# A scan layer's prelude: the convolution as shifted additions on VectorE, two softplus put behind the first scans

## The reference, cut to what matters

```python
gate = sigmoid(x @ W2 + b2)                     # x is the normed input; W1, W2 are 128 x 256
u = x @ W1 + b1
u_pad = pad(u, 3 zeros ahead of the sequence)
u = sigmoid(sum(u_pad[:, k:k + 512, :] * conv_w[:, k] for k in range(4)) + conv_b)
xp = u @ x_proj_w                               # 64 + 16 + 16 columns
delta = softplus(xp[..., :64] @ dt_proj_w + dt_proj_b)
B, C = xp[..., 64:80], xp[..., 80:]
for each time t:                                # 256 channels, 16 states
    h = exp(delta * A) * h + delta * B * u      # A = -exp(A_log)
    y = sum over the states of h * C
out = (y + u * D_skip) * gate @ Wo + bo
```

## Time and profile before

| | us |
|---|---|
| median of three runs (lowest, highest) | 1510.48 (1509.72, 1516.7) |
| the profiled execution | 1518.01 |
| its span, first to last instruction | 1516.2 |
| TensorE busy in the span | 1255.5 |
| VectorE busy | 1024.5 |
| ScalarE busy | 727.8 |
| GpSimd busy | 627.7 |
| first scan of the first layer starts at | 82.26 |
| last instruction of VectorE in the first layer (L609) ends at | 306.14 |

### The profile page before, as it was taken

The page is one execution under the profiler, slowest core; times in us unless marked ns, Lnnn a source line. Parts: engine busy times, 40 slices in busy tenths (PEclk is TensorE's granted clock), DMA queues, the critical chain, the costliest instruction groups (busy, mean ns, idle before and its releaser), DMA issues. The chain is left out here.

```text
span 1516.2 us, 30869 instructions
## 1 busy us (share of the span) xinstructions
PE 1255.5 (83%) x11646; PEld 684.2 (45%) x11674; DVE 1024.5 (68%) x2274; ACT 727.8 (48%) x1593; POOL 627.7 (41%) x838
## 2 busy tenths in 40 slices
PE   7856677769999988547878989987989699999976
PEld 3312233222333337424656666665767333333276
DVE  3699999978888855357446745545632588988653
ACT  2843334316766675313523614443452166766754
POOL 1378888753425215313423334223332524351244
PEclk9978888869999998757889968988997699999988
DMA  4379833023224022441321131141120231331213
GB/s 120 137 264 375 300 137 140 21 66 86 54 65 111 23 80 62 102 85 23 80 40 29 35 83 20 25 100 21 18 52 10 66 81 28 97 88 45 79 48 89
DMA packets 137738, 128.43 MB, mean 85 GB/s; under 512 B 92007, under 2 KB 123559, under 8 KB 132202
## 3 DMA queue, kind: packets, MB, share of 16 engines
q1 hardware_dynamic: 129536, 118.56, 28.3%
q0 software_dynamic: 2496, 5.13, 1.1%
q10 hardware_dynamic: 5558, 2.76, 0.9%
HBM read 105.61 MB, written 38.62 MB: 95 GB/s over the span
## 5 line engine op out<-in xcount | busy, mean ns | idle before, releaser
L1343 DVE TENSOR_REDUCE f_row_min<-f_ps 128x1 f32<-128x512 f32 x512 | 324.4, 677 | 61.2 <-PE f_ps L1670 61.0
L1233 ACT ACTIVATE f_e<-f_ps 128x512 f32<-128x512 f32 x512 | 282.9, 602 | 131.6 <-PE f_ps L1690 128.6
L1670 PE MATMUL f_ps<-f_operands 72*128 72x512 bf16 x512 | 205.1, 409 | 30.0 <-DMA f_operands<-k_scr 16.1
L1690 PE MATMUL f_ps<-f_operands 75*128 75x512 bf16 x512 | 190.5, 382 | 2.6 <-ACT f_e L1233 2.1
L740 PE MATMUL m_ps<-m_shared,sb_ident 128*128 128x512 f32 x256 | 140.2, 698 | 50.8 <-DVE m_shared L596 49.0
L359 POOL TENSOR_TENSOR m_drive<-m_du,m_ring 128x1024 f32<-128x1024 f32 x64 | 150.9, 2372 | 52.7 <-DVE m_ps L588 33.3
L476 ACT ACTIVATE m_ps<-m_delta,m_A 128x511 f32<-128x511 f32 x128 | 83.0, 681 | 129.5 <-DVE m_ps L588 104.8
L1701 PE MATMUL f_ps<-f_e,f_v_op 128*32 128x512 f32 x1024 | 138.0, 611 | 2.1 <-ACT f_e L1233 1.4
L1670 PEld LDWEIGHTS f_ps<-f_operands 72*128 72x128 bf16 x512 | 51.6, 101 | 185.6 <-DVE f_row_min L1343 130.5
L2495 DVE TENSOR_REDUCE d_row_min<-d_ps 128x1 f32<-128x384 f32 (+3 forms) x176 | 106.3, 633 | 37.8 <-PE d_ps L2736 36.8
L2664 DVE TENSOR_TENSOR d_aT<-d_ps,d_aT 128x16 f32<-128x16 f32 x224 | 37.9, 169 | 138.5 <-PE d_ps L2842 138.1
(11 more groups left out here) (291 smaller groups left out, 2343.5 us busy)
## 6 DMA issues: line engine op xcount, KB each, us to landing
m_ring<-bc_scr SPq DMA_DIRECT2D x32, 1024.0 KB, 6.8
f_rows_scr<-blank SPq DMA_DIRECT2D x2, 8707.5 KB, 33.0
f_wall<-f_wall SPq DMA_DIRECT2D x16, 578.0 KB
f_operands<-q_scr SPq DMA_DIRECT2D x32, 288.0 KB
f_operands<-k_scr SPq DMA_DIRECT2D x96, 96.0 KB
d_q_op<-q_scr SPq DMA_DIRECT2D x6, 576.0 KB
d_k_op<-k_scr SPq DMA_DIRECT2D x18, 192.0 KB
f_operands<-f_rows_scr SPq DMA_DIRECT2D x46, 64.5 KB, 1.8
```

Source lines behind the costliest of these rows:

```text
L1233: nc.scalar.activation(e_sb[:, n % 3, hh, :], ps[:, SCORE[(b * UNITS + u) % SCORE_BANKS], :], ACT.Exp, scale=SCALE).then_inc(s["e_out"], 1)
L1343: nc.vector.tensor_reduce(row_min[:, b % 2, u // TPB, u % TPB:u % TPB + 1], ps[:, MAXQ[(b * UNITS + u) % MAX_BANKS], :], AX.X, ALU.max, ne ...
L1670: nc.tensor.matmul(ps[:, MAXQ[n % MAX_BANKS], :], q_op(b, QK)[:, hd, t * P:(t + 1) * P], k_op(b, QK)[:, hd, :], start=True, stop=True).the ...
L1690: nc.tensor.matmul(ps[:, SCORE[n % SCORE_BANKS], :], k_op(b, QKS)[:, hd, t * P:(t + 1) * P], q_op(b, QKS)[:, hd, :], start=True, stop=True ...
```

## The change

The convolution leaves TensorE. `project_u` becomes one product per half with W1 itself. ScalarE copies the result with the bias b1 from PSUM into `du` (`raw`), VectorE multiplies it by the last tap and adds the other three taps times the shifted columns (`convolve`: two tensor_scalar and six scalar_tensor_tensor of 512 columns per batch, or a few columns fewer), and `inputs` takes the sigmoid from SBUF in place, with conv_b as its bias. The product of weights and taps, the edge product and two loads are gone. The orders of VectorE, ScalarE and TensorE in the prelude are written anew. `softplus(2)` and `softplus(3)` move on VectorE behind the output of step 0, and ScalarE takes the two logarithms ahead of the decays of step 2.

```diff
@@ ScalarE
-                act.dma_start(taps, core.dram["m_taps"].unsqueeze(0).to_broadcast([P, CONV_K * MLP])).then_inc(s["taps_in"], 16)
-                load("m_edge", "taps_in")
+                def raw(b):
+                    act.wait_ge(s["u_ps"], b + 1)
+                    for k in range(HALVES):
+                        last = nc.scalar.activation(du[:, k, tokens(b)], bank(U_IN + k), ACT.Identity, bias=vec(core, "b1", k))
+                    last.then_inc(s["raw_out"], 1)
+
                 def inputs(b):
-                    act.wait_ge(s["u_ps"], b + 1)
-                    act.wait_ge(s["u_bias_out"], 1)
+                    act.wait_ge(s["conv_step"], (b + 1) * CONV_STEPS)
                     for k in range(HALVES):
-                        last = nc.scalar.activation(u[:, k, tokens(b)], bank(U_IN + k), ACT.Sigmoid, bias=u_bias[:, k:k + 1])
+                        last = nc.scalar.activation(u[:, k, tokens(b)], u[:, k, tokens(b)], ACT.Sigmoid, bias=vec(core, "conv_b", k))
                     last.then_inc(s["u_out"], 1)
@@ ScalarE's list, after the change
+ turned(0) raw(0) gates(0) turned(1) raw(1) inputs(0) turned(2) raw(2) gates(1) turned(3) raw(3) inputs(1) steps(0)
+ gates(2) decline(0) steps(1) logarithm(0) inputs(2) inputs(3) gates(3) decline(1) steps(2) logarithm(1) steps(3)
+ decline(2) decline(3), then the decays, with
+                        if step == DEFERRED_AT + 1:
+                            for later in DEFERRED:
+                                logarithm(later)
@@ VectorE
+                def convolve(b):
+                    done = b * CONV_STEPS
+                    dve.wait_ge(s["raw_out"], b + 1)
+                    for back in range(CONV_K):
+                        for k in range(HALVES):
+                            tap = vec(core, "conv_w", k * CONV_K + CONV_K - 1 - back)
+                            if back == 0:
+                                nc.vector.tensor_scalar(u[:, k, tokens(b)], du[:, k, tokens(b)], tap, None,
+                                                        ALU.mult).then_inc(s["conv_step"], 1)
+                            else:
+                                dve.wait_ge(s["conv_step"], done + (back - 1) * HALVES + k + 1)
+                                held = u[:, k, b * S + back:(b + 1) * S]
+                                nc.vector.scalar_tensor_tensor(out=held, in0=du[:, k, b * S:(b + 1) * S - back], scalar=tap, in1=held,
+                                                               op0=ALU.mult, op1=ALU.add).then_inc(s["conv_step"], 1)
@@ VectorE's list, after the change
+ norm(0) skip_weights() A norm(1) convolve(0) norm(2) convolve(1) projections(0) norm(3) projections(1) convolve(2)
+ one_plus(0) convolve(3) projections(2) softplus(0) one_plus(1) projections(3) softplus(1) memset
+ one_plus(2) one_plus(3), then the scans, with
+                    if step + 1 == DEFERRED_AT:
+                        for later in DEFERRED:
+                            softplus(later)
@@ TensorE
                     if b >= 1:
-                        pe.wait_ge(s["u_out"], b)
+                        pe.wait_ge(s["raw_out"], b)
                     for k in range(HALVES):
-                        for j in range(CONV_K):
-                            nc.tensor.matmul(bank(U_IN + k), tap_W[:, j, cols], xnT[b % 2][:, j:j + S], start=(j == 0), stop=False)
-                        last = nc.tensor.matmul(bank(U_IN + k)[:, 0:CONV_K - 1], edge_w[:, cols], edge[:, 2 * MLP:],
-                                                start=False, stop=True)
+                        last = nc.tensor.matmul(bank(U_IN + k), W1[:, k * P:(k + 1) * P], xnT[b % 2][:, CONV_K - 1:],
+                                                start=True, stop=True)
@@ TensorE's list, before, then after the change (u, gate, rows, dt: project_u, project_gate, project_rows, project_dt)
- turn(0) u(0) turn(1) gate(0) u(1) turn(2) rows(0) gate(1) dt(0) u(2) turn(3) rows(1) gate(2) dt(1) u(3) rows(2) gate(3)
- dt(2) rows(3) dt(3)
+ turn(0) u(0) gate(0) turn(1) u(1) turn(2) u(2) gate(1) rows(0) turn(3) u(3) dt(0) gate(2) rows(1) dt(1) gate(3) rows(2)
+ dt(2) rows(3) dt(3)
```

More of the change, by code:

```diff
@@ L263, in mamba_phase @@
         W1, W2, Wx, Wdt, Wo = (core.w[n] for n in ("m_W1", "m_W2", "m_xp", "m_dt", "m_Wo"))
-        taps, edge = ring[:, RING - 1, 0, :, :].rearrange("p r s -> p (r s)"), core.w["m_edge"]
         f_hn = gate[:, 0, 0:S].rearrange("p (t h) -> p t h", t=TPB)
@@ L441, in _ @@
                 turned(0)
+                raw(0)
+                gates(0)
+                turned(1)
+                raw(1)
                 inputs(0)
-                turned(1)
-                gates(0)
+                turned(2)
+                raw(2)
+                gates(1)
+                turned(3)
+                raw(3)
                 inputs(1)
-                turned(2)
-                gates(1)
                 steps(0)
+                gates(2)
                 decline(0)
+                steps(1)
                 logarithm(0)
                 inputs(2)
-                turned(3)
-                gates(2)
-                steps(1)
-                decline(1)
-                logarithm(1)
                 inputs(3)
                 gates(3)
+                decline(1)
                 steps(2)
+                logarithm(1)
+                steps(3)
                 decline(2)
-                steps(3)
                 decline(3)
-                logarithm(2)
-                logarithm(3)
                 act.wait_ge(s["a_ready"], 1)
@@ L552, in _ @@
                 norm(0)
-                taps_and_biases()
+                skip_weights()
                 dve.wait_ge(s["a_exp"], 1)
@@ L556, in _ @@
                 norm(1)
+                convolve(0)
                 norm(2)
+                convolve(1)
                 projections(0)
                 norm(3)
+                projections(1)
+                convolve(2)
                 one_plus(0)
-                projections(1)
+                convolve(3)
+                projections(2)
                 softplus(0)
                 one_plus(1)
-                projections(2)
+                projections(3)
                 softplus(1)
-                projections(3)
                 dve.wait_ge(s["gate_out"], B)
                 nc.vector.memset(ps[:, 0:2 * HALVES * S].rearrange("p (a s) -> p a s", s=S)[:, :, 0:1], 0.0).then_inc(s["decay_zeroed"], 1)
-                one_plus(2)
-                one_plus(3)
-                softplus(2)
-                softplus(3)
+                for later in DEFERRED:
+                    one_plus(later)
                 dve.wait_ge(rows_out[B - 2], 16)
@@ L2967, in build @@
         mamba_weights = ExitStack()
-        later = ("in_L0_attn_a_x", "ones", "pad", "f_wall", "blank", "m_taps")
+        later = ("in_L0_attn_a_x", "ones", "pad", "f_wall", "blank")
         for name, a in sorted(arrays.items(), key=lambda item: item[0].startswith("m_")):
```

69 lines of the change are left out of this document (29 added, 40 removed).

## The result

The changed kernel takes 1521.82 us (median of 4 runs, 1517.97 to 1527.16), the kernel before in the same session 1510.1 (4 runs, 1508.06 to 1516.7). The ratio is 1.0082, with an interval of 1.0047 to 1.0117: 0.8% slower. The forecast was 1525.2.

The account below looks back on a forecast made before the run. Layer end was taken as first-scan start plus VectorE's full list behind it. First scan +4.8, moved softplus +7.4 and collision +2.5 gave +14.7 us: 1532.7 for the profiled execution, 1525.2 for the median, range 1512 to 1531.

Parts of the forecast that it names:

- The first scan at 87.0: End of the prelude, from stepping through the engines' queues: first scan at 87.0 us against 82.26, +4.8 us.
- softplus(1) fits in before, to 80.3: VectorE late in the prelude: softplus of batch 1 ends at 80.3 us, before one_plus(3) ends at 87.0.
- Five slow bursts worth 7.2 together: TensorE's prelude: lower-clock products on the path cost 7.2 us; at the upper clock the first scan comes at 79.9.
- Rival (a): TensorE's prelude: gaps stay short and the clock holds, -2.4 + 9.9 = +7.5 us, total 1518.0; chance 0.17.
- (c): Prelude and scans: first scan at 79 to 82 us, GpSimd out of the way, total 1511 to 1517; chance 0.16.
- (d): Prelude: convolutions at their upper price and slow products throughout, total 1531 to 1535; chance 0.10.
- Everything later waits for norm(3): Prelude queues: turn(3) and raw(3) stand ahead of other batches' work, so all later work waits for norm(3), ending at 40.2.
- Convolution 4.4 to 4.5 us per batch: VectorE's prelude: each batch's convolution costs 4.4 to 4.5 us (4.4 to 5.3), 18 in all.
- Softplus moved: +7.4, collision +2.5 (0 to 3.7): Behind the first scan: six products of batches 2 and 3 add 7.4 us to VectorE, colliding with GpSimd for 2.5.
- Logarithms and table loads between decays at nothing: ScalarE between decays of steps 1 and 2: two logarithms and two table loads, 4.7 us, hidden beside VectorE's work.
- Rival (b): Prelude: VectorE runs almost without waiting, first scan at 62.3 us, -10 us, total 1500.4; chance 0.07.
- Whatever moves the first scan moves the end by as much: Scan stretch: VectorE's list is full from the first scan, so any shift of it passes fully to the layer's end.

Follow-up runs that it names:

- the kernel with the clock held: Changed kernel with TensorE's prelude gaps filled by 52 unused products up to the next real product; first scan 82.12 us, layer end 315.47 us.
- the reordered kernel: Changed kernel with VectorE, ScalarE and TensorE prelude queues in other orders and no deferral of softplus and logarithms; ratio 0.9981 to the kernel before.
- the run with one tap: Changed kernel with three of the four convolution taps left out, 16 us less VectorE work; first scan 2.45 us earlier.
- after: The changed kernel as profiled, against the kernel before; median 1521.82 us, ratio 1.0082.
- The reordered kernels: Changed kernel with new queue orders and no deferral: alone (0.9981), with GpSimd's bias additions later (1501.07 us), and also with drives 1 to 3 delayed (first scan 68.72 us).
- the drives held back: New queue orders, no deferral, later bias additions, plus GpSimd's drives 1 to 3 waiting for the last softplus; first scan 68.72 us, layer end 296.58 us.

## Why the prediction was right

The time was forecast as 1525.2, +14.7; measured is +11.7 in the medians and +13.9 at the end of the layer. Sign and size came out, by the mechanism that was called likeliest. Luck has a part in how closely: the clock alone moved the copy for batch 1 from 50.94 to 56.63 us between executions, and the mis-sized terms below partly cancel. By its steps:

- **"The first scan at 87.0" (+4.8): 87.59.** The way there was right too. The copies for batches 0 to 3 stand at 32.35, 50.94, 65.80 and 73.95 where the walk has 32.8, 51.1, 65.6 and 74.5. (The sign given for it, VectorE idle some 5 us ahead of the copies of batches 0 and 1, did not fit the walk itself, which has 4.9 and 10.9; measured are 3.5 and 11.3.) The last link was partly another: the walk ends through ScalarE's decline(3), but one_plus(2) starts at 83.83, when the last stretched product of softplus(1) ends, half a microsecond after decline(2) at 83.3.
- **"softplus(1) fits in before, to 80.3": mis-sized.** Its three products took 2.17, 3.25 and 3.25, 5.0 us of stretching for some 1.0 allowed. It ended at 83.9. VectorE, idle in the walk, is full from 65.8 us on. It cost only 0.6 us here because ScalarE was just as late; in the kernel with the clock held it is what keeps the first scan at 82.12 and not at the 79.9 of the same walk at full clock.
- **"Five slow bursts worth 7.2 together": mis-sized.** Right in kind: four products on the path took 3.4 to 3.8 us. Of the walk's five, W1(1) ran at the upper level (1.99 us). Measured by filling TensorE's gaps they are worth 5.5 us. Rival (a), the clock holds, would have needed a filled queue; the run that filled it gives its mechanism but ended the layer only 3.9 us earlier, 5.8 if the last gate's longer wait is set aside. Rivals (c) and (d) needed a first scan at 79 to 82 or slow products throughout; neither is in the trace.
- **"Everything later waits for norm(3)": half right.** turn(3) did wait 7.39 us for it. But moving norm(3) alone gave 2.0 us, since the clock took back the rest; it is the order of all three queues that costs (16.7 us by the reordered kernel), and norm(3) is one place of it.
- **Convolution 4.4 to 4.5 us per batch: mis-sized.** It is 4.76, 0.66 for each scalar_tensor_tensor of 512 columns instead of 0.62. It hardly matters, as the run with one tap showed: 16 us less of it gave 2.45.
- **Softplus moved: +7.4, collision +2.5 (0 to 3.7).** The block measured 10.7 us, so the collision is 3.3, near the upper bound. 2.1 us came back behind it, 1.3 of that in VectorE's waits at the gates and the last addition (6.4 instead of 7.7), so the stretch grew by 8.6 where 9.9 was forecast.
- **Logarithms and table loads between decays at nothing: right.** They end ahead of VectorE's scan 1. The Trainium skill's page "ScalarE: Activation LUTs", section "What ACT_TABLE_LOAD costs", speaks of 1.38 us more per load, by which the forecast would have been 5.5 higher. The trace disagrees: in after, the activation follows the load 0.01 to 0.02 us after its end, as before.
- **Rival (b), the prelude really shrinks**, which needed the first scan before 64.8, had the right condition, and in the changed kernel's order it was not met. The reordered kernels show that the potential was there. They have all four softplus ahead of the scans; less the 7.3 us of two of them, an estimate, their first scans would stand at 72.2, 67.7 and, with the drives held back, 61.4 us, against the rival's 62.3. What the order frees goes first to GpSimd's collisions.
- **"Whatever moves the first scan moves the end by as much"** held well enough for the change, but it is no law of this kernel: the drives held back moved the first scan by 6.3 us and the end of batch 0 by nothing (129.41 against 129.23), for behind it stood the ring's chunk and not VectorE's list.

Open are what sets the clock's different course in executions of the same instructions, and whether moving the 8.7 MB transfer would free the end of batch 0.

## What to carry to other kernels

Work taken off the busiest engine gives nothing until the other queues are put in a new order: here TensorE lost 25 us, VectorE gained 19, and the prelude with the same softplus in it became 14 us longer (96.25 against 82.26 us); the order of the queues alone was worth some 17. When a gain in front disappears behind, look for what stands there besides the busy engine. An engine that stops being the bound also loses what its density gave, here the upper clock, 5.5 us; look at the first product behind each new gap. And before an engine is told to wait so as not to collide, ask what its next products release: the drives held back here gave 6 us in front and took as much by the end of batch 0, since the first output product came later, and with it a large transfer and the chunk queued behind it.

## What the runs showed of the hardware that was not expected

- Small products (128 by 32 weights, 256 columns), two records of some 0.22 us each, held TensorE's granted clock at 1.00 from 18 to 71 us when they filled the gaps: W1(3) took 1.98 us behind them, and 3.58 behind a gap of 3.4 us.
- The same instructions get the lower or the upper level at different times in different executions: the copy for batch 1 stood at 50.94, 52.30 and 56.63 us in three executions whose instructions are the same up to there.
- Collisions of VectorE with GpSimd come in a few sizes: a 1.22 us product takes 2.14 to 2.17, 2.61 or 3.24 to 3.27, a 0.70 us one 2.73 to 2.83, and GpSimd's four drives take 12.59 us instead of 9.3 undisturbed.
- A chunk of 1 MB issued behind a transfer of 8.7 MB in the same queue landed 28 to 32 us after its issue, where the quickest took 4.8; it landed at the same distance behind the large transfer whether it was issued 1.0 or 5.3 us after it (first use 33.4 and 33.7 us behind).
